# Attention plus mixture of experts: the last norms, gates and the routing moved beside the attention, constants awaited one by one, stacks written once, expert results fetched tile by tile

## The reference

```
xn  = layernorm(x)
att = softmax(rope(q) rope(k)^T / sqrt(8), causal, |i-j| <= 64) v      # 16 heads of 8
y   = att @ Wproj.T + bproj
gates = xn @ gate_w.T + gate_b                                        # 8 experts
w, idx = top_k(gates, 2); w = softmax(w)
moe = sum_e  w_e * (gelu(xn @ w1[e] + b1[e]) @ w2[e] + b2[e])         # 128 -> 512 -> 128
out = x + y + moe
```

## Time and profile before

| | |
|---|---|
| median of the runs | 835.83 us (835.56 to 837.29, 3 runs) |
| profiled execution | 834.06 us, of which the span of the profile is 832.0 us |
| PE busy | 721.6 us (87%) |
| DVE busy | 475.0 us (57%) |
| ACT busy | 365.1 us (44%) |
| POOL busy | 367.0 us (44%) |
| DMA | 151.19 MB, mean 182 GB/s |

### The profile page before, as it was taken

The page is one execution under the profiler, slowest core; times in us unless marked ns, Lnnn a source line. Parts: engine busy times, 40 slices in busy tenths (PEclk is TensorE's granted clock), DMA queues, the critical chain, the costliest instruction groups (busy, mean ns, idle before and its releaser), DMA issues.

```text
span 832.0 us, 25812 instructions
## 1 busy us (share of the span) xinstructions
PE 721.6 (87%) x9815; PEld 590.3 (71%) x9816; DVE 475.0 (57%) x1330; ACT 365.1 (44%) x685; POOL 367.0 (44%) x507
## 2 busy tenths in 40 slices
PE   1678767999999999989989599999999999999286
PEld 0567445666666666666666399999999999998164
DVE  6334697676676666666766344444444444444483
ACT  0243223555545545555555344444444444445244
POOL 2465203333333433334334146555655566554550
PEclk9955577999999999999999799999999999999789
DMA  9756333565566656655655687788788777872894
GB/s 269 264 167 197 93 95 108 154 165 154 150 161 159 155 151 158 165 143 154 170 152 147 165 223 211 218 221 218 215 213 218 221 215 213 216 215 74 273 267 141
DMA packets 163825, 151.19 MB, mean 182 GB/s; under 512 B 30296, under 2 KB 131800, under 8 KB 163704
## 3 DMA queue, kind: packets, MB, share of 16 engines
q1 hardware_dynamic: 149536, 128.37, 57.0%
q0 software_dynamic: 8640, 17.97, 6.7%
q10 hardware_dynamic: 5528, 3.20, 1.6%
HBM read 91.69 MB, written 57.70 MB: 180 GB/s over the span
## 4 chain that ended last, share of the span: by engine, by line
PE 66%; issue 12%; ACT 7%; DVE 6%; DMA 3%; POOL 3%; ACTq 2%; SPq 0%; DVEq 0%; POOLq 0%
PE ps L565 17%; PE ps L578 15%; PE ps L404 4%; PE ps L513 4%; PE ps L496 3%; PE ps L434 3%; PE ps L485 2%; PE ps L457 2%; PE ps L450 2%; ACT Os L918 2%; PE ps L389 2%; PE ps L425 2%; PE ps L551 2%; PE ps L415 2%; PE ps L541 2%
## 5 line engine op out<-in xcount | busy, mean ns | idle before, releaser
L982 POOL DMA_INDIRECT slots_x<-xn,pos x128 | 126.9, 991 | 251.9 <-DVE mx L761 235.6
L761 DVE TENSOR_REDUCE mx<-ps 128x8 f32<-128x1024 f32 x128 | 156.8, 1225 | 119.8 <-PE ps L457 119.6
L911 ACT ACTIVATE PT<-ps 128x1024 f32<-128x1024 f32 x128 | 131.9, 1031 | 194.7 <-PE ps L496 194.6
L932 ACT ACTIVATE hb<-ps,b1b 128x256 f32<-128x256 f32 x284 | 119.0, 470 | 169.5 <-PE ps L565 166.6
L988 POOL DMA_INDIRECT chosen_y<-xn,to x142 | 137.8, 970 | 48.0 <-issue 30.1
L565 PE MATMUL ps<-xn 128*128 128x256 f32 x568 | 153.1, 413 | 0.0
L578 PEld LDWEIGHTS ps<-xn,hb 128*128 128x128 f32 x1136 | 139.1, 193 | 1.8
L565 PEld LDWEIGHTS ps<-xn 128*128 128x128 f32 x568 | 139.1, 328 | 0.5
L578 PE MATMUL ps<-xn,hb 128*128 128x128 f32 x1136 | 138.1, 275 | 0.0
L513 PE MATMUL ps<-PT,V 128*32 128x64 f32 (+1 forms) x3072 | 84.1, 243 | 0.2 <-ACT PT L911 0.2
L450 PE MATMUL ps<-cb_s 64*64 64x512 bf16 (+1 forms) x384 | 54.0, 421 | 29.2 <-issue 14.9
(11 more groups left out here) (123 smaller groups left out, 926.4 us busy)
## 6 DMA issues: line engine op xcount, KB each, us to landing
xn<-in_w SPq DMA_DIRECT2D x142, 256.0 KB
QK<-stack SPq DMA_DIRECT2D x128, 192.0 KB
stack<-sp SPq DMA_DIRECT2D x64, 192.0 KB
slots_x<-hb SPq DMA_DIRECT2D x22, 426.0 KB, 4.9
xn<-slots_x SPq DMA_DIRECT2D x71, 132.0 KB, 3.7
stack<-sp SPq DMA_DIRECT2D x64, 128.0 KB
xn<-chosen_y SPq DMA_DIRECT2D x32, 256.0 KB, 5.4
xn<-in_b SPq DMA_DIRECT2D x71, 64.0 KB
```

The costliest lines, as they stand in the source:

```text
L761: e.tensor_reduce(mo[:, :, :, c, t], ps[:, 0:2, :].rearrange("p g (h k) -> p g h k", k=P), AX.X, ALU.max, negate=True).then_inc(v_mx, 1)
L911: e.activation(PT[:, u % 2, :], ps[:, 2:4, :].rearrange("p c k -> p (c k)"), ACT.Exp, scale=SCALE).then_inc(a_exp, 1)
L932: e.activation(hb[:, s, c, :], ps[:, 2 * s + c // 2, (c % 2) * SL:(c % 2 + 1) * SL], ACT.Gelu, bias=b1b[:, i % NW, c:c + 1]).then_inc(a_ge ...
L982: e.indirect_dma_start(out=Xs, out_offset=bass.IndirectOffsetOnAxis(ap=pos[:, n, u:u + 1], axis=0), in_=xn[:, u, :], in_offset=None).then_ ...
```

## The change

- Groups: the last seven groups of 8 become five of 8 (up to tile 48) and four of 4 (`GR`, `NB` = 7). The first five take four values of q each (statistics, apply, turn, gates, and the gate sum at the fourth, right ahead of the next group's statistics); the last four run beside units, at q = -3 to 14. Gate products and gate sums are separate steps (`gates` on PE, `gsum` on DVE). The gate sums of groups 0 and 1 stand ahead of the statistics of group 2.
- Unit 0 waits for seven gate sums and no longer for the routing.
- Routing in nine parts at q = 16 to 19 and 21 to 25, its two products at q = 20 and 21, in PSUM bank 5. The scatters stand at q = 27 to 100.
- Constants: semaphores of their own for the identity and for `wqkv`.
- x is loaded group by group from q = -19 on behind the first four groups; the 22 clearing DMAs go one to each q.
- The stack has three term slots a side and is written by one DMA. The load repeats them: twelve DMAs instead of four.
- `CUT` is 25: the experts come after unit 100. The fetches are one to each q, three ahead of their combine.

```diff
-CUT = 27
+CUT = 25
-GR = (0, 4, 8, 16, 24, 32, 40, 48, 56, 64)
+GR = (0, 4, 8, 16, 24, 32, 40, 48, 52, 56, 60, 64)
+NB = 7
+ROUTE = 16
+    def normal(q):
+        j = q - FIRST
+        for g in range(2, NG):
+            j0 = 4 * (g - 2) if g < NB else 18 + 4 * (g - NB)
+            if j == j0 - 6 and 3 < g < NB or j == j0 - 4 and g >= NB:
+                order.append(("xload", g))
+            if j == j0:
+                order.extend([("stats", g), ("norm", g)])
+            if j == j0 + 1:
+                order.append(("apply", g))
+            if j == j0 + (2 if g < NB else 3):
+                order.append(("turn", g))
+            if j == j0 + (3 if g < NB else 4):
+                order.append(("gates", g))
+            if j == j0 + (4 if g < NB else 5):
+                order.append(("gsum", g))
+        if q == ROUTE + 4 or q == ROUTE + 5:
+            order.append(("count", q - ROUTE - 4))
+        if ROUTE <= q < ROUTE + 4 or ROUTE + 5 <= q < ROUTE + 10:
+            order.append(("route", q - ROUTE - (q > ROUTE + 3)))
...
-            order.extend([("fetch", b) for b in range(NF)])
...
+        if 4 <= q - FIRST < 4 + NZ:
+            order.append(("clear", q - FIRST - 4))
+        k = q - (4 * CUT + 2)
+        if 0 <= k < NP:
+            order.append(("fetch", k))
+        if 0 <= k - 3 < NP:
+            order.append(("combine", k - 3))
...
-    Dst = [nc.dram_tensor(f"stack_{i}", (2, 6, P, 256), bf16).ap() for i in range(3)]
+    Dst = [nc.dram_tensor(f"stack_{i}", (2, 3, P, 256), bf16).ap() for i in range(3)]
...
-                    for d0, n in ((0, 3), (3, 2), (5, 1)):
-                        e.dma_start(Dv[0, :, d0:d0 + n, :], sp[:, s, 0, 0:n, :]).then_inc(d_w[b % 3], 16)
-                    for d0, n, s0 in ((0, 3, 0), (3, 2, 1), (5, 1, 2)):
-                        e.dma_start(Dv[1, :, d0:d0 + n, :], sp[:, s, 1, s0:s0 + 1, :].broadcast_to(
-                            (P, n, 256))).then_inc(d_w[b % 3], 16)
+                    e.dma_start(Dst[b % 3].rearrange("a m c t -> c (a m) t"),
+                                sp[:, s, :, :, :].rearrange("p a m t -> p (a m) t")).then_inc(d_w[b % 3], 16)
...
                     for i in range(2):
-                        Dv = Dst[b % 3][i].rearrange("s (d h) t -> (s d) (h t)", h=16)
-                        for g in range(2):
-                            e.dma_start(QK[64 * g:64 * g + 48, s, i, :],
-                                        Dv[:, g * 2048:(g + 1) * 2048]).then_inc(d_r[s], 16)
+                        Dv = Dst[b % 3][i].rearrange("m (d h) t -> m d (h t)", h=16)
+                        for m, n in enumerate((3, 2, 1)):
+                            r0 = 8 * (0, 3, 5)[m]
+                            for g in range(2):
+                                src = Dv[m:m + 1] if i else Dv[0:n]
+                                if i and n > 1:
+                                    src = src.broadcast_to((n, 8, 4096))
+                                e.dma_start(QK[64 * g + r0:64 * g + r0 + 8 * n, s, i, :],
+                                            src[:, :, g * 2048:(g + 1) * 2048]).then_inc(d_r[s], 16)
...
-                        e.wait_ge(v_gate, NG)
-                        e.wait_ge(v_rt, 18)
+                        e.wait_ge(v_gate, NB)
...
-            for o, i in ((cf_s[:, 0:128], cf[:, 0:128]), (gw_s[:], gate_w), (wq_s[:], wqkv),
-                         (gb_s[:], gate_b.partition_broadcast(P)), (cf_s[:, 128:], cf[:, 128:])):
+            e.dma_start(cf_s[:, 0:128], cf[:, 0:128]).then_inc(d_i, 16)
+            e.dma_start(wq_s[:], wqkv).then_inc(d_q, 16)
+            for o, i in ((gw_s[:], gate_w), (gb_s[:], gate_b.partition_broadcast(P)), (cf_s[:, 128:], cf[:, 128:])):
                 e.dma_start(o, i).then_inc(d_c, 16)
```

More of the change, by code:

```diff
@@ L25, in schedule @@
 def schedule():
-    order = [("stats", 0), ("norm", 0), ("turn", 0), ("stats", 1), ("norm", 1), ("turn", 1)]
+    order = [("stats", 0), ("norm", 0), ("turn", 0), ("stats", 1), ("norm", 1), ("turn", 1), ("gates", 0), ("gsum", 0),
+             ("gates", 1), ("gsum", 1)]
     first = ((), (("less_mid", 15), ("proj", -9)), (), ())
@@ L66, in schedule @@
         put(late, q)
[L67 to L82, removed]
+        normal(q)
+        if 4 <= q - FIRST < 4 + NZ:
+            order.append(("clear", q - FIRST - 4))
         while moved < 2 * NT and moved * (4 * CUT - routed) < 2 * NT * (q - routed):
@@ L86, in schedule @@
             moved += 1
[L87 to L96, removed]
+        k = q - (4 * CUT + 2)
[3 more added lines that the diff above has]
+            order.append(("combine", k - 3))
+            if (CUT + k - 3) % NP < CUT:
+                order.append(("store", (CUT + k - 3) % NP))
+        if (q - 10) % 4 == 0 and CUT <= (q - 10) // 4 < NP:
+            order.append(("store", (q - 10) // 4))
     return order
@@ L218, in semaphore @@
             return ctx.enter_context(nc.semaphore(name))
-        d_c, d_k, d_z = (semaphore(n) for n in ("d_c", "d_k", "d_z"))
+        d_i, d_q, d_c, d_k, d_z = (semaphore(n) for n in ("d_i", "d_q", "d_c", "d_k", "d_z"))
         d_x = [semaphore(f"d_x{g}") for g in range(NG)]
@@ L268, in xn_ready @@
                 return v_xn, u + 1
-            return (p_xn, 4 * (u // 8 - 1) + u % 8 + 1) if u % 8 < 4 else (a_xn, 4 * (u // 8 - 1) + u % 8 - 3)
+            g = max(i for i in range(NG) if GR[i] <= u)
+            h, before = (GR[g + 1] - GR[g]) // 2, (GR[g] - 8) // 2
+            return (p_xn, before + u - GR[g] + 1) if u - GR[g] < h else (a_xn, before + u - GR[g] - h + 1)
         def v3(t):
@@ L698, in _ @@
                         k.then_inc(v_rt, 1)
-                    elif part == 5:
+                    elif part == 6:
                         e.wait_ge(v_rt, 19)
@@ L856, in _ @@
                     e.wait_ge(p_nrm, PNRM * (g - 1))
-                    for u in range(GR[g] + 4, GR[g + 1]):
+                    for u in range((GR[g] + GR[g + 1]) // 2, GR[g + 1]):
                         e.activation(xn[:, u, 0:P], xr[:, u, :], ACT.Identity, bias=nb[:, u:u + 1],
@@ L967, in _ @@
                     e.wait_ge(p_nrm, PNRM * (g - 1))
-                    for u in range(GR[g], GR[g] + 4):
+                    for u in range(GR[g], (GR[g] + GR[g + 1]) // 2):
                         e.tensor_scalar(xn[:, u, 0:P], xr[:, u, :], mv[:, u, 0:1], rs[:, u:u + 1], ALU.subtract,
```

63 lines of the change are left out of this document (38 added, 25 removed).

## The result

| | before | after |
|---|---|---|
| median of the runs beside each other | 835.69 us (4 runs) | 901.0 us (893.92 to 912.05, 4 runs) |
| profiled execution, its span | 834.06, 832.0 us | 912.05, 910.0 us |
| PE busy | 721.6 us (87%) | 749.0 us (82%) |
| written to HBM | 57.70 MB | 45.12 MB |

The change makes the kernel slower: ratio 1.0752, interval 1.0658 to 1.0847. The profiled execution is the longest of the four and was in a slower state than the other three (893.92 to 905.63 us), which alone make the ratio; its stretches add up to 78 us and not to 65, so e2 and e7 are used beside it where the size matters.

What follows compares the result with a forecast made beforehand. PE was taken as the bound, about 3.18 us a unit, with DVE the bound during early routing. 0 + 7 + 10.5 + 22 - 8 = +31.5 on 834.06 gave 865.6 profiled, 867 us timed; range for 8 in 10: 827 to 900.

Steps and rivals of the forecast that it cites:

- the narrow k-side load: Stack load: k-side sources with a small outer size run on few engines, 34 rows on the busiest; +22 us.
- 0 + 7 + 10.5 - 12: Terms without the load's cost: start 0, small groups +7, routing +10.5, tail -12 us.
- Stack written once: Stack write and load: halved write gains 0, twelve-DMA load takes 10.4 us against a 9.2 us window; +22 us.
- 1.2 us of wait in each batch: PE waits for the late load in each of 18.5 batches from unit 26 to 100; +22 us.
- The shape of the load: Stack load: outer source size limits the k side's engines; busiest carries 34 k-side rows and about 8 q-side rows.
- rival 3: Stack load: both sides narrow, 68 rows on the busiest engine, 5.2 us wait a batch; +90, 955 us; chance 0.08.
- rival 1: Stack load: spread over engines or fitting its window, so no wait; 841 us timed; chance 0.20.
- Start, 0: Stretch up to unit 12: the longer group chains and the routing moved out cancel; 0 us (-5 to +5).
- Rival 2: Whole kernel faster: load hidden, small groups and routing fit idle time, PE's clock high before unit 0; 829 us; chance 0.21.
- Small groups +7: Four groups of 4 beside early units: extra PE and DVE work and waits; +7 us (+3 to +11).
- routing +10.5: Routing parts in units 16 to 25: DVE becomes the bound and nothing hides it; +10.5 us (+6 to +15).
- Tail, -8: Behind the experts: fetch gap goes, -16; late loads +4 and nine combines left +4; -8 us (-15 to 0).

Runs made afterwards that it cites:

- e2: The kernel before with only the new stack (three term slots, one write, twelve loads); 892.59 us, ratio 1.0687.
- e7: The kernel after with the k side of each load issued first; 894.75 us, ratio 1.0695.
- e1: The kernel after with the old stack (six term slots, six writes, four loads of 48 rows); 843.46 us, ratio 1.0107.
- e3: The kernel before with each load cut into twelve transfers of 24, 16 and 8 rows from a flat source; 835.2 us, ratio 0.9996.
- e8: The kernel after with every k-side repeat its own 8-row transfer, 18 in all; 845.93 us, ratio 1.0126.
- e12: The kernel after with the doubled k-side term as single transfers, 30 rows on the busiest engine, on a slower chip; ratio 1.0558 to before.
- e6: The kernel before with only norms, gates, routing, scatters, x loads, clears and constants moved (old stack, fetches at once, CUT 27); 855.07 us, ratio 1.0238.
- e17: The kernel after itself, unchanged, on a slower chip; ratio 1.0572 to before.
- e14: The kernel before with one fetch to each q and CUT 25, on a slower chip; ratio 0.9947 to before.

## Why the prediction was right or wrong

The direction and the mechanism were right, and so was which term is the largest: the narrow k-side load is the loss. The size was wrong: +65 us where +31 was forecast, 901.0 just outside a range that ended at 900. The rest without the narrow load was forecast at 0 + 7 + 10.5 - 12 = +5.5 and measured at +7.5 (e1). The step that failed is **"Stack written once"**, the term "1.2 us of wait in each batch", +22: measured were 2.1 us a batch in e2 and 2.8 in after.

- *Stack written once, +22.* From unit 28 to 100 measured +37.7 in e2, +42.5 in e7 (271.5 us) and +50.3 in the profiled execution of after. Two parts are off. First, the load is longer than 10.4 us: on the mean of the loads from 230 to 510 us the product comes 12.4 us behind the first issue in after and 11.9 in e2. By its packets the first k row starts at 4.0 us (forecast 3.4), the k rows last 7.6 us in after and 7.1 in e2 (forecast 6.5), and the product comes 0.8 us behind the last row (the 0.5 of the sum had no row behind it). A row alone is as quick as I took it, or quicker, 0.16 us in the median. But over the whole stretch the busiest engine works off its 34 k rows at 0.21 to 0.22 us each, since single rows took over 1 us and rows do not follow without gaps; what held them is not shown. From its first row to its last it has 42 rows (34 + 8) in 10.7 us, 0.25 each, and in e7 in 9.5 us, 0.23 each: nearer to the 0.27 of a loaded engine in the earlier trace rows than to my 0.19. Second, I priced the wait and nothing behind it. PE's busy time for a batch grew from 11.6 to 12.5 us (12.3 in e2), since 7 of 12 waits bring the lower clock to the products behind them: a third of the loss, for which the sum had no term.
- *The shape of the load.* The count of packets confirms it. q1 has 149536 packets before and 123520 after. The two more loads of x that after puts on it add 32, so 26048 went, 814 a batch. In e2, without these two loads, q1 has 123488: the same 26048. The write of half the bytes has 768 rows fewer; six writes have 96 completion entries and one has 16; four loads had 64. 768 + 80 + 64 - 98 = 814: the twelve loads have 98. That is 2 x (12 + 16 + 8) for the q side with 24, 16 and 8 rows joined, and 2 x (3 + 2 + 8) for the k side. The other loads count up in the same way: 144 for the twelve wide ones of e3 (2560 packets more than before, 80 a load), 168 in e8 (2240 more than after, 70 a load), 126 in e12 (896 more, 28 a load). So the k side is narrow and the q side wide; rival 3 is out, and rival 1 too, since e8, with the same data in transfers without a repeat, stands at 1.0126 and not at 1.0752. By the Trainium skill ("DMA: Bandwidth & Descriptors", "Why a DMA increments its semaphore by 16 and not by 1") the number of engines is the largest up to 16 that divides the slowest size on both sides; all four sums agree with it, and so do the three rows and the two rows at a time in the packets.
- *Start, 0.* Right at the point named, in part by luck: the maximum of unit 12 starts at 129.22, forecast 129 (130.32 in the earlier trace rows). But the seventh gate sum ends at 120.4, forecast 116.3, and unit 10's maximum starts at 122.73, forecast 121: the chain of the groups was 4 us longer than forecast and what follows it as much shorter. In e6 unit 12 comes at 126.40. Rival 2's condition, a fast PE in this stretch, failed: the granted clock was 0.67 from 95.8 to 129.7. The rows of after's DVE:

```profile
120.16 0.21 DVE L666 TENSOR_TENSOR G<-ps,gb_s 128x64 f32<-128x64 f32 x1
...
122.73 1.23 DVE L790 TENSOR_REDUCE mx<-ps 128x8 f32<-128x1024 f32 x1 [0.36 <-PE ps L486]
...
129.22 1.22 DVE L790 TENSOR_REDUCE mx<-ps 128x8 f32<-128x1024 f32 x1
```

and its stretches of units 16 to 26 and of the start, as in the earlier trace rows:

```profile
182.40:222.10 39.70, 32.42 (x619) 21.89 (x616) 34.30 (x74) 17.67 (x30) 0.00 (x0) 0.91 0.29 82
...
95.80:129.70 33.90, 27.43 (x266) 19.05 (x267) 20.73 (x67) 10.82 (x20) 11.65 (x38) 0.67 0.50 164
```

- *Small groups +7, routing +10.5.* With the start's -1.1 us taken out, unit 16 is late by 182.36 - 173.95 + 1.1 = 9.5 us, forecast 7 (bounds 3 to 11), and units 16 to 28 take 53.4 us against 38.1, +15.3, forecast 10.5 (bounds 6 to 15). In e6 they are 14.0. I had charged 1.5 us for uneven parts. DVE was expected above 90% busy and was 89% in e6 and 86% in after (34.25 of 38.40 and 34.30 of 39.70 us): by this I put the idle time between uneven parts at some 4 us, and batch 24 to 27 was the worst. The load costs nothing here, as forecast: unit 28 comes at 232.90 us in e6, which has the old stack, and at 232.84 in e7. It does cost where no routing makes the batches longer: e2 takes 43.6 us from unit 16 to 28 (178.36 to 221.95), before 38.1.
- *Tail, -8.* Measured -3.7 + 6.9 = +3.2, the other way. Without narrow loads (e1) the last 26 units take 68.5 us and the end 17.4 against 85.3 and 10.4, -9.8 where I had -16 + 4 = -12. The gap is gone, and nine combines stand behind unit 127, both as forecast. The narrow loads of the last six batches cost 81.6 - 68.5 = 13.1 us, not 4: I charged only two of them. That is the mis-sized load again.

## What to carry to other kernels

Before you turn one DMA into one with a leading repeat or a small outer size, count the rows on its busiest engine over the whole of what one consumer waits for, and take the loaded price of a row (here 0.23 to 0.25 us for 4096 bytes, where a row alone takes 0.16); the bytes saved on the other side are worth nothing if that queue had slack. Price a new wait of a PE-bound stretch as the wait plus the products that follow it at the lower clock (here half as much again). If a step is spread behind a cut, count what is left behind the last unit, and move the cut with it.

## What the runs showed of the hardware

- A PE that stood 2.2 us on the mean (39.0 us in 18 batches) once in 15.5 us was granted 0.93 of its clock on the mean, against 1.00 with 1.1 us of idle in pieces: after 413.70 the same four products took 0.41, then 0.64 us, at a granted 0.50.
- A row of 4096 bytes took 0.16 us (median in after, e2, e7, e8, e12 and e17). A transfer with an outer source size of 3 moved three rows at a time, one of 2 two rows.
- The form of the source set the width, not its bytes: the same 8-row blocks took 843 to 846 us of kernel time as four wide or 18 small transfers (e1, e8) and 895 to 901 (e7, after) as twelve, of which the four with a repeat ran on three or two engines. The last row landed 5.3 and 8.2 us behind the first issue in the first two, 11.1 and 11.6 in the others.
- Chips differ. Before took 836 us in three sets of runs and 889, 893 and 889 us on three other chips. On one of these e14 made 3164 products from 250 to 450 us where before, above, made 3833, and its granted clock was still 0.96:

```profile
250.00:450.00 200.00, 166.93 (x3164) 113.60 (x3163) 110.40 (x195) 90.86 (x145) 67.86 (x69) 0.96 0.50 131
```

  PE was idle 33.1 us of the 200, against 17.5, with no wait for a load over 1 us, and a product took 52.8 ns and not 47.6 on the mean. Their cause was not found, and the same change cost 5.7% on another of these chips (e17), not 7.5%.
